# Layer 3 of a four-layer Flamingo block on Trainium2: norm, router, ranks and row scatter as one pipeline of eight groups

## The reference, cut to what matters

```python
xr = layernorm(x).reshape(S, 256)                      # S = 4096
probs = softmax(xr @ Wg, axis=-1)                      # Wg: 256 x 8
gate_vals, expert_idx = top_k(probs, 2)
oh = one_hot(expert_idx.reshape(-1), 8)
pos = sum((cumsum(oh, axis=0) - 1) * oh, axis=1)       # rank of a choice within its expert
kept = pos < 1280                                      # ceil(1.25 * S * 2 / 8)
# rows that are kept go to place pos of their expert; then, per expert:
expert_out = relu(dispatched @ w1) @ w2                # w1: 256 x 1024, w2: 1024 x 256
out = sum over the two choices of gate * kept * expert_out
x = x + tanh(g_ffn[3]) * out
```

## Time and profile before

| what | value |
|---|---|
| median of 3 runs | 4015.32 us (4015.22 to 4018.01) |
| the profiled execution: its own time | 4010.64 us |
| the profiled execution: span from first to last instruction | 4008.6 us |
| mean granted TensorE clock over the span | 0.856 |
| busy share: PE, PEld, DVE, ACT, POOL | 72%, 45%, 57%, 37%, 22% |
| instructions of one execution | 60740 |

### The profile page before, as it was taken

One profiled execution on the slowest core, in us unless ns is written; L12 is line 12 of the kernel. 1 busy time (PEld: TensorE's weight loads), 2 busy tenths in 40 slices (PEclk: granted clock), 3 DMA queues, 4 the chain that ended last, 5 costly groups with the idle time before them and its releaser, 6 DMA issues. The chain is left out here.

```text
span 4008.6 us, 60740 instructions
## 1 busy us (share of the span) xinstructions
PE 2881.3 (72%) x19894; PEld 1816.7 (45%) x19894; DVE 2286.4 (57%) x4602; ACT 1469.7 (37%) x2927; POOL 868.9 (22%) x1207
## 2 busy tenths in 40 slices
PE   5388864565999955797166973688869716999993
PEld 5133324222555533233133752344447615888883
DVE  7699975575777766334686977555569630000003
ACT  5277751352222244797143541111135301112110
POOL 3011111573333354111001320000023142111110
PEclk7599995897999975899587986899989758999997
DMA  7766611996222244882001421100024121121113
GB/s 252 169 120 120 120 52 38 350 356 255 81 80 80 81 133 127 137 119 33 23 0 59 139 73 42 40 10 10 12 98 138 33 101 45 58 67 51 55 53 127
DMA packets 270503, 394.33 MB, mean 98 GB/s; under 512 B 57345, under 2 KB 197870, under 8 KB 269984
## 3 DMA queue, kind: packets, MB, share of 16 engines
q1 hardware_dynamic: 243408, 321.15, 30.0%
q0 software_dynamic: 25152, 68.22, 4.9%
q10 hardware_dynamic: 1680, 1.57, 0.2%
HBM read 231.94 MB, written 164.44 MB: 99 GB/s over the span
## 5 line engine op out<-in xcount | busy, mean ns | idle before, releaser
L2581 POOL DMA_INDIRECT rows_out<-e_out,e_tr_dest x224 | 234.5, 1047 | 870.7 <-DVE e_out L3204 508.8
L1183 ACT ACTIVATE a_pt<-a_psS 128x512 f32<-128x512 f32 x512 | 277.5, 595 | 155.4 <-PE a_psS L1081 151.0
L3204 DVE COPY e_out<-e_psD 128x512 f32<-128x512 f32 x40 | 27.6, 691 | 491.9 <-PE e_psD L3172 491.7
L1205 DVE TENSOR_REDUCE a_mx_sb<-a_psM 128x4 f32<-128x1024 f32 x256 | 292.9, 1213 | 18.9 <-PE a_psM L1064 17.7
L2972 PE MATMUL e_psG<-e_wgu,e_yT 128*128 x576 | 275.0, 600 | 25.7 <-ACT e_yT L3000 23.1
L1095 PE MATMUL a_psV<-a_pt,a_vt 128*18 128x256 f32 x4096 | 292.0, 387 | 1.2 <-issue 0.8
L3172 PE MATMUL e_psD<-e_w,e_hT 128*128 128x256 f32 x1280 | 289.7, 386 | 0.0
L3161 PE MATMUL e_psH<-e_yT,e_w 128*128 128x256 f32 x1280 | 284.5, 381 | 1.6 <-issue 0.8
L3104 ACT ACTIVATE e_hT<-e_psH 128x512 f32<-128x512 f32 x160 | 95.5, 597 | 452.0 <-PE e_psH L3161 452.0
L3172 PEld LDWEIGHTS e_psD<-e_w,e_hT 128*128 128x128 f32 x1280 | 245.5, 194 | 33.1
L3161 PEld LDWEIGHTS e_psH<-e_yT,e_w 128*128 128x128 f32 x1280 | 244.1, 191 | 35.5 <-issue 2.1
(11 more groups left out here) (376 smaller groups left out, 5908.9 us busy)
## 6 DMA issues: line engine op xcount, KB each, us to landing
kbd<-e_bgu SPq DMA_DIRECT2D x64, 512.0 KB, 5.0
cr_kbd<-kbd SPq DMA_DIRECT2D x64, 512.0 KB, 3.4
rows_in<-zeros POOLq DMA_DIRECT2D x36, 522.0 KB, 6.3
e_xin<-rows_in SPq DMA_DIRECT2D x144, 128.0 KB
vbd<-e_bd SPq DMA_DIRECT2D x64, 272.0 KB, 3.7
cr_vbd<-vbd SPq DMA_DIRECT2D x64, 272.0 KB, 2.7
cq_rows<-rows_out SPq DMA_DIRECT2D x32, 512.0 KB, 5.8
e_w<-in_L_ffn_w_dram SPq DMA_DIRECT2D x16, 1024.0 KB, 7.8
```

The source lines that it names most:

```text
L1183: act.activation(pt[:, probs(t, h), b, :, :], psS[:, unit(t, h, b) % S_BANKS, :].rearrange("p (k c) -> p k c", k=KC), ACT.Exp, scale=scale ...
L1205: dve.tensor_reduce(mx[:, t % 2, :, h, :], psM[:, k % 2, :, :].rearrange("p b (f c) -> p b f c", f=2), AX_X, ALU.max).then_inc(ring_read, 1)
L2581: pool.indirect_dma_start(out=self.rows_out[0:limit, :], out_offset=bass.IndirectOffsetOnAxis(ap=self.dest[:, t:t + 1], axis=0), in_=rows, ...
```

## The change

`phase_norms`, `phase_project`, `phase_slots` and `phase_scatter` of layer 3 are replaced by one block, `phase_route_scatter`. The 32 tiles go through it in eight groups of four (`G`, `NG`). Statistics and the power -1/2 are taken for eight tiles at a time; the first two such batches come before all else. The normed rows of a group are written once, into one of three buffers (`RING`), turned and multiplied from there, and scattered from there. Ranks come from products of eight columns: for tile j of a group one with the triangular matrix, j with the matrix of ones over the earlier tiles of the group, and one with the counts carried from earlier groups (14 products per group, accumulated in PSUM). DVE's order is `choose(i)`, `normed_rows(i + 2)`, in two groups `statistics`, `place(i)`, `carry_on(i)`; `place(i)` releases the eight indirect DMAs of group i on POOL. SP loads the router weights and then prefetches the expert weights at the start of the block. The capacity test, the weights and the row numbers are the same as before. The other layers keep the old functions.

```diff
@@ -2531,6 +2531,256 @@
...
+def phase_route_scatter(core, w_router, weight, rows_in, limit, mark, gate, prefetch):
...
+    E, K, G, RING = 8, 2, 4, 3
+    NG = TILES // G
...
+    sent = [core.lasting_sem(f"{n}s{u}") for u in range(RING)]
...
+        y = sb(ctx, n + "y", [P, RING, G, ROW], F32)
+        yT = sb(ctx, n + "yT", [P, 2, 2, KC, P], F32)
...
+        index = [sb(ctx, f"{n}i{u}", [P, G, K], U32) for u in range(RING)]
...
+                sp.dma_start(wr[:, :, :], w_router.rearrange("(k p) e -> p k e", p=P)).then_inc(w_loaded, 16)
+                prefetch(sp)
...
+                def root(h):
+                    pool.wait_ge(eased, h + 1)
+                    both = slice(2 * h * G, 2 * (h + 1) * G)
+                    pool.tensor_tensor(core.rstd[:, both], vareps[:, both], core.half[:, 0:2 * G], ALU.pow).then_inc(rooted, 1)
+                root(0)
+                root(1)
+                for g in range(NG):
+                    pool.wait_ge(placed, g + 1)
+                    for j in range(G):
+                        for k in range(K):
+                            pool.indirect_dma_start(out=rows_in[:, :], out_offset=bass.IndirectOffsetOnAxis(ap=index[g % RING][:, j, k:k + 1], axis=0),
+                                                    in_=y[:, g % RING, j, :], in_offset=None, bounds_check=limit - 1, oob_is_err=False).then_inc(sent[g % RING], 16)
+                    if g % 2 == 0 and g // 2 + 2 < NG // 2:
+                        root(g // 2 + 2)
+                for u in range(RING):
+                    pool.wait_ge(sent[u], 16 * G * K * ((NG - u + RING - 1) // RING))
...
+                def turn(g):
+                    for j in range(0, G, 2):
+                        i = (g * G + j) // 2
+                        pe.wait_ge(y_ready, g * G + j + 2)
+                        if i >= 2:
+                            pe.wait_ge(y_copied, i - 1)
+                        for v in range(2):
+                            for k in range(KC):
+                                at = (v * KC + k) * P
+                                ins = pe.transpose(psT[:, i % 2, at:at + P], y[:, g % RING, j + v, k * P:(k + 1) * P], core.ident[:, :])
+                        ins.then_inc(y_turned, 1)
...
+                def route(g):
+                    if g >= 2:
+                        pe.wait_ge(lg_ready, g - 1)
+                    for j in range(G):
+                        i = (g * G + j) // 2
+                        pe.wait_ge(y_copied, i + 1)
+                        for k in range(KC):
+                            ins = pe.matmul(psL[:, g % 2, j * E:(j + 1) * E], yT[:, i % 2, j % 2, k, :], wr[:, k, :], start=(k == 0), stop=(k == KC - 1))
+                        if j % 2:
...
+                def count(g):
+                    pe.wait_ge(masked, g + 1)
+                    pe.wait_ge(carried, g)
+                    if g >= 1:
+                        pe.wait_ge(multiplied, g)
+                    for j in range(G):
+                        out = psR[:, j * E:(j + 1) * E]
+                        pe.matmul(out, before[:, :], mask[:, g % 2, j, :], start=True, stop=False)
+                        for earlier in range(j):
+                            pe.matmul(out, ones[:, :], mask[:, g % 2, earlier, :], start=False, stop=False)
+                        ins = pe.matmul(out, ones[:, :], carry[:, g % 2, :], start=False, stop=True)
+                    ins.then_inc(ranked, 1)
...
+                for i in range(NG + 2):
+                    if 0 <= i - 2:
+                        count(i - 2)
+                    if i < NG:
+                        turn(i)
+                        route(i)
...
+                for i in range(NG + 1):
+                    if i < NG:
+                        for h in range(G // 2):
+                            p = i * (G // 2) + h
+                            act.wait_ge(y_turned, p + 1)
+                            if p >= 2:
+                                act.wait_ge(routed, p - 1)
+                            act.activation(yT[:, p % 2, :, :, :], psT[:, p % 2, :].rearrange("p (t k c) -> p t k c", t=2, k=KC), ACT.Copy).then_inc(y_copied, 1)
+                        act.wait_ge(routed, (i + 1) * (G // 2))
...
+                        act.activation(lg[:, i % 2, :, :], psL[:, i % 2, 0:G * E].rearrange("p (t e) -> p t e", t=G), ACT.Copy).then_inc(lg_ready, 1)
+                    if 0 <= i - 1:
+                        act.wait_ge(lowered, 2 * (i - 1) + 2)
+                        act.activation(ex[:, :, :], ex[:, :, :], ACT.Exp).then_inc(exped, 1)
+                        act.activation(exall[:, :, :], exall[:, :, :], ACT.Exp).then_inc(exped, 1)
...
+                def statistics(h):
+                    tiles = range(2 * h * G, 2 * (h + 1) * G)
+                    for t in tiles:
+                        dve.bn_stats(stats[:, t, :], core.xs[:, t, :]).then_inc(surveyed, 1)
+                    for t in tiles:
+                        dve.wait_ge(surveyed, t + 1)
+                        dve.bn_aggr(core.mv[:, t, :], stats[:, t, :]).then_inc(averaged, 1)
+                    dve.wait_ge(averaged, tiles[-1] + 1)
+                    both = slice(tiles[0], tiles[-1] + 1)
+                    dve.tensor_scalar(vareps[:, both], core.mv[:, both, 1], LN_EPS, None, ALU.add).then_inc(eased, 1)
+                def normed_rows(g):
+                    dve.wait_ge(rooted, g // 2 + 1)
+                    if g >= RING:
+                        dve.wait_ge(sent[g % RING], g // RING * (16 * G * K))
+                    for j in range(G):
+                        t = g * G + j
+                        dve.tensor_scalar(y[:, g % RING, j, 0:DIM], core.xs[:, t, :], core.mv[:, t, 0:1], core.rstd[:, t:t + 1],
+                                          ALU.subtract, ALU.mult).then_inc(y_ready, 1)
+                def choose(g):
+                    v = g % 2
+                    dve.wait_ge(lg_ready, g + 1)
+                    for j in range(G):
+                        dve.max(top[:, j, :], lg[:, v, j, :]).then_inc(topped, 1)
+                    for j in range(G):
+                        dve.wait_ge(topped, g * G + j + 1)
+                        dve.max_index(idx[:, j, :], top[:, j, :], lg[:, v, j, :]).then_inc(indexed, 1)
+                    dve.tensor_tensor(ex[:, :, :], top[:, :, 0:K], each(top[:, :, 0], K), ALU.subtract).then_inc(lowered, 1)
+                    dve.tensor_tensor(exall[:, :, :], lg[:, v, :, :], each(top[:, :, 0], E), ALU.subtract).then_inc(lowered, 1)
+                    dve.wait_ge(indexed, (g + 1) * G)
+                    c = Chain(dve, number_step, g, 2)
+                    c.link(dve.tensor_copy(idxf[:, v, :, :], idx[:, :, :]))
+                    for k in range(K):
+                        ins = dve.tensor_tensor(hot[:, v, k, :, :], iota[:, :].rearrange("p (a e) -> p a e", a=1).broadcast_to([P, G, E]),
+                                                each(idxf[:, v, :, k], E), ALU.is_equal)
+                    c.link(ins)
+                    c.close()
+                    dve.wait_ge(lowered, 2 * g + 2)
+                    dve.tensor_tensor(mask[:, v, :, :], hot[:, v, 0, :, :], hot[:, v, 1, :, :], ALU.add).then_inc(masked, 1)
...
+                def carry_on(g):
+                    v = g % 2
+                    dve.wait_ge(masked, g + 1)
+                    dve.tensor_reduce(part[:, :], mask[:, v, :, :].rearrange("p t e -> p e t"), AX_X, ALU.add).then_inc(counted, 1)
+                    dve.wait_ge(counted, g + 1)
+                    if g >= 1:
+                        dve.wait_ge(ranked, g)
+                        dve.wait_ge(carried, g)
+                    dve.tensor_tensor(carry[:, 1 - v, :], carry[:, v, :], part[:, :], ALU.add).then_inc(carried, 1)
+                def place(g):
...
+                    dve.wait_ge(exped, 2 * g + 2)
+                    c.link(dve.tensor_reduce(den[:, 0, :], exall[:, :, :], AX_X, ALU.add))
+                    c.link(dve.reciprocal(den[:, 1, :], den[:, 0, :]))
+                    c.link(dve.tensor_tensor(ex[:, :, :], ex[:, :, :], each(den[:, 1, :], K), ALU.mult))
+                    dve.wait_ge(ranked, g + 1)
+                    for k in range(K):
+                        ins = dve.tensor_tensor(tmp[:, k, :, :], hot[:, v, k, :, :], psR[:, 0:G * E].rearrange("p (t e) -> p t e", t=G), ALU.mult)
+                    ins.then_inc(multiplied, 1)
+                    dve.wait_ge(multiplied, g + 1)
+                    for k in range(K):
+                        ins = dve.tensor_reduce(rank[:, :, k], tmp[:, k, :, :], AX_X, ALU.add)
+                    c.link(ins)
+                    c.link(dve.tensor_scalar(kept[:, :, :], rank[:, :, :], float(CAPACITY), None, ALU.is_lt))
+                    c.link(dve.scalar_tensor_tensor(out=weight[:, group(g), :], in0=ex[:, :, :], scalar=gate, in1=kept[:, :, :], op0=ALU.mult, op1=ALU.mult))
```

(15 more changed lines are left out.)

81 lines of the change are left out of this document (added).

## The result

The changed kernel takes 3984.83 us (median of 3 runs, 3978.35 to 3987.74) against 4015.32; the ratio is 0.9923 with a 95% interval of 0.9907 to 0.994. It is faster, by 30.5 us between the medians; 3987.0 was predicted. The profiled execution took 3987.74 us, its span is 3986.0 and the mean granted clock 0.855.

What follows compares the result with a forecast made beforehand. Four phases in single file, 181.4 us, bound the kernel; the new block, with sends and placing alternating, takes 153.2. The 28.2 us less gave 3982.4 for the profiled execution, 3987.1 for the median; range 3970 to 4004.

Steps and rivals of the forecast that it cites:

- What bounds: Layer 3's norms to the experts' first fetch (the stage): four phases in single file, 181.4 us; savings shorten the end.
- Start: New block's start to first send, 28.2 us: statistics, normed rows, transposes and router products to 18.9, then ranks and placing.
- One term at nothing: Block start: POOL's constants were said to lie under the 28 us before the first send.
- The ranks: `count` in each group: 14 products of 0.43 us, 6.0 us in all, hidden under the sends in the steady part.
- rival D: New block's PE work: clock rises to 2.4 GHz, 14.6 us saved on turning, routing and three counts, 3972; chance 0.03.
- The period: Steady part, i = 1 to 5: sends and placing alternate, 16.7 us each, 3.4 more at i = 2 for statistics.
- The end: Groups 6 and 7, which fill no buffer: sends begin at 125.6 and 136.1 us; last send to experts' fetch 8.1.
- Rival B: Sends: a true stream, POOL never waits after the first send; 120.3 us, 61 us less, 3954; chance 0.05.
- Rival C: Sends: DVE and POOL block each other, 14.7 us added over seven groups, 4002; chance 0.08.
- Rivals E and F: Waits for landings: E, 7.1 us each, 4010, chance 0.05; F, eight sends queue, at 11 us 4029, chance 0.04.

Runs made afterwards that it cites:

- e7: Changed kernel with four buffers, five count products and a reordered start: 3945.89 us, ratio 0.9822 to the kernel before, stage 111.2 us.
- e3: Changed kernel with the 14 count products issued twice per group: 4013.25 us in one run, stage 172.4 us.
- e5: Changed kernel, still three buffers, with five count products per group instead of 14: 3983.23 us in one run, stage 148.0 us.
- e8: Changed kernel run again unedited: 3979.87 us in one run, stage 152.6 us.
- e1: Changed kernel with four buffers instead of three: 3952.16 us, ratio 0.9848 to the kernel before, stage 122.6 us.
- e2: Changed kernel, still three buffers, with normed_rows(i + 2) moved last in DVE's order: 3964.51 us in one run, stage 144.1 us.
- e4: Changed kernel, still three buffers, with statistics put before normed_rows(i + 2) in groups 0 and 2: 3985.47 us in one run, stage 148.8 us.
- e6: Changed kernel with four buffers and five count products per group: 3948.95 us, ratio 0.9835 to the kernel before, stage 115.9 us.
- e9: Changed kernel with six fp32 copies of 128x1024 added on DVE beside the sends, groups 1 to 5: 3994.45 us in one run, stage 160.6 us.

## Why the prediction was right

By its own steps:

- **What bounds.** Every microsecond of the stage is one off the end: what follows it took the same time, within 1.1 us, in the two profiles compared.
- **Start.** 28.2 predicted, 27.4 measured. Eight transposes take 1.78 us from their start to the start of the router products (3169.43 to 3171.21 on PE), not 2.2: the 1.11 us of four run from the first start to the last end, and that end overlaps what follows. This was counted twice and is the 0.8. The power of eight columns takes 1.67 us, the value on the line between the two ends.
- **One term at nothing was wrong.** POOL's constants were said to lie under the 28 us. DVE waits for all of them before its first statistics:

```profile
3161.50 0.29 POOL L2600 TENSOR_SCALAR_AFFINE_SELECT rs_before<-rs_before 128x128 f32<-128x128 f32 x1
...
3161.82 2.71 DVE L2697 BATCH_NORM_STATS2 rs_stats<-xs 128x6 f32<-128x256 f32 x8 [2.21 <-POOL rs_before L2600]
```

  The block's idle before the first `bn_stats` is 2.21 us where it was 1.21, so 1.0 us was lost ahead of the stage. e7 moves the wait and has 1.20 again.
- **The ranks.** 14 products in 6.0 us, as costed; hidden in groups 1 to 5 and in the open at the start, by e3. In groups 6 and 7 they are in the open, but only 0.5 us each can be had back, by e5: the prediction's price for rival D (18 us of counts on the path, half of them saved) was too high, since the sends stood right beneath. This doesn't enter the forecast.
- **The period.** 16.7 predicted; 16.5 to 16.7 measured for three of the five, 17.2 in the first, where DVE was released 3.04 us after the last start (3198.32 to 3201.36) instead of 2.61. With the statistics 20.1 predicted and 20.2 measured. In e8 the first was 16.8, so that 0.4 comes and goes. e1, e2 and e4 each took one part of this period away, and the stage came out within 0.9 us of what was expected.
- **The end.** 10.5 us from group to group predicted, 10.7 measured; from the last send to the experts 8.1 both times.
- **Rival B**, the true stream, is what the kernel becomes with one buffer more and fewer products: in the prediction it had 92.1 us from first send to fetch (120.3 - 28.2), and e6 has 92.3.
- **Rival C.** The changed kernel's sends stayed at 0.97 us in the middle beside DVE's small instructions. In e9 large copies stretched them by 0.2 to 0.4. The Trainium skill, SBUF — State Buffer, section "A bandwidth-pool intuition that's wrong (but worth ruling out)", gives about 0.62 us alone against about 3.1 overlapped with a DVE copy for a DMA issued from POOL's queue. These rows agree that such a copy reaches POOL's sends; no issue in the stages of these runs was over 1.35 us. The skill's figures are for the whole DMA and the rows' for its issue, and no copy of e9 was longer than 0.7 us, so the size of the effect that it gives is not tested.
- **Rival D.** The clock was 0.50 from the first statistics to the end of the stage, also in e3. The Trainium skill, TensorE: Matmul & The Clock Gate, Part 1, has a busy array at full clock; these rows disagree for fp32 transposes and products of eight columns.
- **Rivals E and F.** Landings took 3.1 us at the most with eight sends in flight (3.6 in e1 and e2). In the old scatter the first three sends, beside the weights' prefetch, landed in 6.4 to 7.1 us, and those from 3262 on in 2.2 to 2.7. Now the prefetch ends before the first send: the DMA engines are busy 0.99 up to 3172 and 0.14 from there to 3189.

The median came out at 3984.83 for a predicted 3987.1. That closeness is partly luck: the stage was right within 0.2 us, but over the ten profiles the part ahead of it moved by 16 us and the part behind it by 6. The profiled execution alone, put at 3982.4, took 3987.74.

## What to carry to other kernels

A ring of buffers is judged by what stands behind its wait on the same engine, not by its depth alone: here the refill waited in front of the step that feeds the consumer, and with three buffers POOL and DVE still took turns. Walk the engine's order with the wait's condition in hand and write down the period; then either add the one buffer (30 us here) or put the feeding step first (9 us). When a term is taken off a path, look for the next one under it before booking the gain: nine products less in three places were worth 5.1 us and not 11.6.

## What the runs showed of the hardware that was not expected

- TensorE was granted 0.50 of its clock over 120 us in which it was busy 92% with fp32 products of 128x8 and transposes of 128x128 (e3), while the experts' 256-column fp32 products got 0.92 over their first 61 us and 1.00 from 3400 to 3500 us, busy 94% in both.
- An fp32 copy of 128x1024 in SBUF takes DVE some 0.7 us (six in 4.33), about half of what 256-column instructions had suggested. Beside such copies the issue of an indirect DMA on POOL takes 1.13 to 1.35 us in place of 0.97 (e9).
- Products of up to 32 columns, some with an operand repeated by a zero stride, cost the same 0.43 us as those of eight: five in place of fourteen saved 3.8 us (e5).
- The unchanged phases ahead of the stage end at times that differ by up to 16 us between executions (3147.1 to 3163.4).
